# Sums and 1/std of four blocks kept in PSUM in the node stage, and half as many short memsets behind the early gathers

## The chip, the cores and the metric

The kernel runs on one core of a Trainium2 chip. A core has TensorE (PE, matrix products and transposes, results in the eight banks of PSUM), VectorE (DVE), ScalarE (ACT), GpSimd (POOL) and SyncE (SP), which run side by side and wait for one another on semaphores, and 16 DMA engines that all queues share. SP issues the plain transfers. GpSimd issues the indirect ones (a gather or a scatter of 128 rows by a list of row numbers). GpSimd and DMA reach SBUF, but not PSUM.

The metric is the time of one launch on the device in microseconds (us).

## The reference

The input is x (100000 nodes of 64 floats), 25000 edges with a source, a destination (sorted) and 64 features, and the weights. Everything is float32.

```
h = relu(layernorm(x))                               # (x - mean) / sqrt(var + 1e-5)
msg_f = mlp_f([h[src], h[dst], edge])                # 192 -> 128 -> 128, relu between
msg_r = mlp_r([h[dst], h[src], edge])
agg   = segment_sum(msg_f, dst) + segment_sum(msg_r, src)
out   = x + h + mlp_n([agg, h])                      # 192 -> 128 -> 64, relu between
```

## The kernel before

The second layer of both edge MLPs is multiplied into the first node weight, so a message is what an edge adds to the hidden layer of a node. A DRAM table holds one row of 128 floats per node: the node's share of its hidden layer, to which the edges' shares are then added.

**Node stage** (0 to about 286 us). 98 blocks ("windows" in the code) of 1024 nodes, 128 partitions by G = 8 nodes by 64 floats. For each, SP loads x into a ring of four buffers `nx` (256 KB), VectorE sums (`sum_begin`, L1056), subtracts the mean (`centre_begin`, L1063), sums the squares that ScalarE makes (`variance_begin`, L1069), inverts ScalarE's square root (`invert_begin`, L1073) and makes h (`normal_begin`, L1080). TensorE transposes h (L764) and multiplies it (L775), ScalarE copies the result out (L683), and SP stores it to the table (512 KB). VectorE's order in one step n is: sum of block n+3, variance of n+2, centring of n+3, inverse of n+2, h of n+2. The sums and 1/std of all blocks stay in SBUF, in `all_sums` and `all_rstd` (128 x 98 x 8), because the edge stage makes h of every block again on ScalarE (`h_window`, L639) from x, -mean/std and 1/std. The steps 4 to 91 are a hardware loop of 22 turns with four steps each.

Beside this GpSimd makes the **early gathers**: for the 98 batches of the edge stage, the x rows of all even batches and of the first three odd ones, 52 x 4 = 208 gathers of 128 rows (L514), into `got_even` and `got_odd`. Behind each of them stands a memset of 128 x 256 floats of `idle`, which is a part of `to_send[0]` (L567). In SBUF the gathers need only the list `gather_first`, so they start at 7.9 us and are issued one after the other, whatever the other engines do. The memset waits for the memset before it, and the two write nothing that anyone reads.

**Edge stage** (to about 1340 us). 98 batches of 256 edges. Per batch: layer norm of the gathered rows on VectorE and ScalarE, transposes (`turn`), first layer (`layer1`), second layer (`layer2`), `messages` on VectorE, `join` on TensorE (L846: adds the messages of a batch that go to the same node), a copy of the result to `to_send` on ScalarE (`copy_sums`, L625), and four scatters on GpSimd that add 128 rows each to the table (L532), with half of the gathers of a later odd batch behind them (L514 again). On TensorE a step is join of batch n-2, turn of n, layer2 of n-1, layer1 of n. On ScalarE a step is root n, relu n-1, half of h_window n, square n+1, copy_sums n-2, copy_turned n, the other half. So what stands behind `copy_sums` of batch 0 on ScalarE is `copy_turned` of batch 2, without which TensorE can't go on with layer1 of batch 2 and all behind it. And `copy_sums` of batch 0 waits for `join` of batch 0 and for all 208 memsets (`act.wait_ge(s_paused, KB * (PAIRS + LOOK))`, L624), since they write into its output. GpSimd's scatters stand behind all early gathers in its own queue.

**Output stage** (to the end). 98 blocks: table in, relu, second node layer, plus x + h, out.

VectorE's setup work in the node stage uses banks 6 and 7: the turned edge numbers (bank 6, L916), w2 turned (bank 7, L744 and L928) and the products of the weights (bank 6, L752 and L932). Banks 0 and 1 hold the transposes, 2 to 5 the products. Apart from the turned w2, bank 7 is not used before the first odd `join` of the edge stage.

## Time and profile before

| | us |
|---|---|
| median of 3 runs (1623.82 to 1632.91) | 1625.49 |
| time of the profiled execution | 1627.22 |
| its span, first to last instruction | 1625.5 |
| early gathers and their memsets, in the span | 7.9 to 339.3 |
| node stage, until its last product is copied out | about 0 to 283 |
| edge stage, from the first scatter to the last | 340.9 to 1354 |
| output stage | to 1625.5 |

Busy shares of the span: PE 81%, DVE 60%, ACT 58%, POOL 69%. They are means over three stages with different limits, so the rows below are read by stage. A row of a timeline gives the start and the length of an instruction in us, its engine, line, operation and operands, how many were merged (x), and in brackets how long its engine had been idle before and what ended that. "issue" is idle time for which the profile shows no releaser.

### The profile page before, as it was taken

To read this page: it belongs to the slowest core of one execution; us is meant where nothing else is said; L and a number is where in the kernel's file an instruction comes from. 1 tells how busy PE (TensorE), PEld (TensorE's weight loads), DVE (VectorE), ACT (ScalarE), POOL (GpSimd) and SP (SyncE) were. 2 spreads that over 40 slices of the span, in tenths; PEclk is the share of its full clock that TensorE was granted. 3 is DMA by queue.
4 is the path that set the end of the run, shared out by engine and by line. 5 is a ranking of instruction groups with operands and counts; after the bars stand their busy time and mean duration, and the time that the engine had idled before them with its cause. 6 is when DMAs were issued, how large, how long until landed. Compare 5 with 4: busy or idle time off the path is not lost.

```text
span 1625.5 us, 29085 instructions
## 1 busy us (share of the span) xinstructions
PE 1318.5 (81%) x7070; PEld 997.1 (61%) x7070; DVE 972.4 (60%) x2902; ACT 944.0 (58%) x2256; POOL 1120.1 (69%) x1003
## 2 busy tenths in 40 slices
PE   6988998457787788887877887878888865899998
PEld 4777776345565666665656665656666654666665
DVE  7999998336666666666665666666666641222222
ACT  5888888244555455555545555455555533677776
POOL 7899878888888888888888888888888862000000
PEclk9999999567878777778787778787777777999999
DMA  7999998335555555555545555555555546999998
GB/s 222 310 312 315 315 312 280 101 59 108 103 109 108 107 104 103 102 103 103 102 93 99 101 103 102 98 100 102 103 103 102 102 76 205 333 369 348 346 349 292
DMA packets 238374, 280.71 MB, mean 173 GB/s; under 512 B 53170, under 2 KB 155200, under 8 KB 238348
## 3 DMA queue, kind: packets, MB, share of 16 engines
q1 hardware_dynamic: 168408, 241.57, 44.7%
q0 software_dynamic: 68992, 38.59, 20.3%
q10 hardware_dynamic: 948, 0.30, 0.1%
q14 instruction: 21, 0.17, 0.0%
q8 instruction: 5, 0.08, 0.0%
HBM read 162.62 MB, written 117.72 MB: 172 GB/s over the span
## 4 chain that ended last, share of the span: by engine, by line
POOL 28%; issue 19%; DMA 15%; PE 9%; DVE 5%; ACT 1%; POOLq 0%; SPq 0%; DVEq 0%; another core or an unknown queue 0%; ACTq 0%
POOL table L532 24%; DMA out_x<-ncentred 12%; POOL got_odd L514 5%; DMA table<-to_send,scatter_at 3%; PE bank L846 3%; DVE ncentred L1137 2%; PE bank L820 2%; PE bank L818 2%; PE bank L833 1%; DVE same L979 1%; PE bank L871 1%; DMA same<-table 1%; PE bank L804 1%; PE bank L882 0%; DVE sums L961 0%
## 5 line engine op out<-in xcount | busy, mean ns | idle before, releaser
L532 POOL DMA_INDIRECT table<-to_send,scatter_at x392 | 640.9, 1635 | 134.1 <-issue 118.3
L846 PEld LDWEIGHTS bank<-message,same 128*128 128x128 f32 x1960 | 300.1, 243 | 47.1 <-issue 43.6
L846 PE MATMUL bank<-message,same 128*128 128x128 f32 x1960 | 322.4, 335 | 3.3 <-DVE message L1010 3.3
L639 ACT ACTIVATE nh<-nx,all_sums,all_rstd 128x64 f32<-128x64 f32 x784 | 280.2, 434 | 0.0
L514 POOL DMA_INDIRECT got_even<-in_x,gather_first x196 | 211.8, 1081 | 40.9 <-issue 36.1
L775 PE MATMUL bank<-wn_h,nturned 128*128 128x256 f32 x784 | 196.6, 394 | 26.9 <-ACT nhidden L683 18.4
L514 POOL DMA_INDIRECT got_odd<-in_x,gather_at x180 | 179.9, 999 | 54.8 <-issue 54.2
L818 PE MATMUL bank<-turned,w_ends 128*128 128x256 f32 x392 | 175.5, 540 | 37.8 <-ACT turned_edge L609 37.1
L804 PE MATMUL bank<-ident,h_ends 128*128 128x128 f32 x196 | 51.4, 355 | 184.4 <-DVE h_ends L1019 181.4
L1004 DVE TENSOR_TENSOR scatter_at<-moved,ids 128x4 int32<-128x4 f32 x98 | 16.0, 163 | 296.6 <-DMA table<-to_send,scatter_at 296.6
L775 PEld LDWEIGHTS bank<-wn_h,nturned 128*128 128x128 f32 x784 | 143.1, 192 | 63.3 <-issue 33.0
L820 PE MATMUL bank<-turned_edge,w_edge 64*128 64x256 f32 x392 | 179.4, 547 | 0.0
L991 DVE CUSTOM_DVE_ANT_0 junk<-same,earlier 128x128 bf16<-128x128 f32 (+3 forms) x392 | 168.9, 487 | 0.0
L713 ACT ACTIVATE nhidden<-bank,bn_col 128x512 f32<-128x512 f32 x196 | 124.0, 684 | 70.2 <-PE bank L871 70.2
L616 ACT ACTIVATE hidden<-bank,b 128x256 f32<-128x256 f32 x196 | 82.1, 470 | 124.3 <-PE bank L820 122.4
L979 DVE TENSOR_SCALAR same<-others,ids 128x128 f32<-128x128 int32 (+3 forms) x392 | 143.7, 429 | 11.7 <-issue 7.6
L804 PEld LDWEIGHTS bank<-ident,h_ends 128*128 128x128 f32 x196 | 28.9, 181 | 195.3 <-issue 195.3
L871 PE MATMUL bank<-ident,same 128*128 128x128 f32 x784 | 108.4, 282 | 38.1 <-DMA same<-table 36.5
L833 PE MATMUL bank<-w2n,hidden 128*128 128x128 f32 x784 | 139.0, 336 | 0.0
L625 ACT COPY to_send<-bank 128x512 f32<-128x512 f32 x98 | 56.6, 577 | 139.4 <-PE bank L846 55.7
L871 PEld LDWEIGHTS bank<-ident,same 128*128 128x128 f32 x784 | 85.4, 143 | 77.5 <-issue 53.7
L820 PEld LDWEIGHTS bank<-turned_edge,w_edge 64*128 64x128 f32 x392 | 75.1, 239 | 94.0 <-issue 94.0
(78 smaller groups left out, 1971.0 us busy)
## 6 DMA issues: line engine op xcount, KB each, us to landing
nx<-in_x SPq DMA_DIRECT2D x194, 256.0 KB
table<-nhidden SPq DMA_DIRECT2D x97, 512.0 KB
same<-table SPq DMA_DIRECT2D x97, 512.0 KB, 5.3
others<-numbers SPq DMA_DIRECT2D x196, 128.0 KB
out_x<-ncentred SPq DMA_DIRECT2D x97, 256.0 KB, 4.4
nx<-out_x SPq DMA_DIRECT2D x55, 256.0 KB, 4.6
out_x<-nh SPq DMA_DIRECT2D x31, 256.0 KB
table<-to_send,scatter_at POOLq DMA_INDIRECT x392
```

The source lines that it names most:

```text
L514: pool.indirect_dma_start(to[:, k * D:(k + 1) * D], None, x, bass.IndirectOffsetOnAxis(ap=numbers[:, k:k + 1], axis=0)).then_inc(landed, 16)
L532: pool.indirect_dma_start(table, bass.IndirectOffsetOnAxis(ap=scatter_at[s][:, k:k + 1], axis=0), to_send[s][:, k, :], None, compute_op=AL ...
L639: last = act.activation(nh[s][:, g, :], nx[place][:, g, :], ACT.Relu, bias=all_sums[:, at, g:g + 1].rearrange("p a g -> p (a g)"), scale=a ...
L713: act.activation(nhidden[s][:, odd * 512:odd * 512 + 512], bank[2 + 2 * s + odd][:, :], ACT.Relu, bias=bn1_col[:, 0:1]).then_inc(n_hidden[ ...
L775: last = pe.matmul(bank[2 + 2 * s + half][:, c:c + 2 * M], nturned[s][:, q * P:(q + 1) * P], wn1_h[:, :, :].rearrange("p a m -> p (a m)"), ...
L818: pe.matmul(bank[2 + s][:, c:c + JT * P], w1_ends[:, end, :], turned[s][:, 0:JT * P], start=True, stop=False)
L820: last = pe.matmul(bank[2 + s][:, c:c + JT * P], w1_edge[:, end, :], turned_edge[s][:, :], start=False, stop=True)
L833: last = pe.matmul(bank[4 + s][:, k * M:(k + 1) * M], hidden[s][:, end, j * P:(j + 1) * P], w2n[:, end, :], start=True, stop=True)
L846: last = pe.matmul(bank[6 + s][:, k * M:(k + 1) * M], same[s][:, o, k * P:(k + 1) * P], message[s][:, o, :], start=(o == k), stop=(o == KB ...
L871: last = pe.transpose(bank[2 + 2 * s + odd][:, q * P:(q + 1) * P], ntab[place][:, g * M:(g + 1) * M], ident[:, :])
L979: last = dve.tensor_scalar(same[s][:, o, 0:w], row[:, 0:w], ids[s][:, o:o + 1], None, ALU.is_equal)
L991: last = dve.tensor_tensor_reduce(junk[s][:, k, 0:w], same[s][:, k, 0:w], earlier[:, KB * P - w:], 1.0, 0.0, ALU.mult, ALU.add, before[s][ ...
```

## The change

VectorE writes the sums and 1/std of a block into one of four places in bank 7 (`some_sums`, `some_rstd`, 8 floats per partition each) instead of `all_sums` and `all_rstd`, and `centre_begin` and `normal_begin` read them there. Once in four blocks a copy (`keep`) moves 4 x 8 sums to `all_sums`, and another one 4 x 8 values of 1/std to `all_rstd`; two new semaphores count them, and the first of the next four blocks waits for them. The setup's turned w2 moves from bank 7 to bank 6, where its transposes wait for the copies of what lay there before. Of the memsets behind the early gathers every second one (k = 0 and 2) goes, and `copy_sums` waits for 104 instead of 208. The start of the edge stage waits for the 25 + 25 copies.

```diff
+        some_sums = bank[7][:, 0:NRING * G].rearrange("p (w g) -> p w g", g=G)
+        some_rstd = bank[7][:, NRING * G:2 * NRING * G].rearrange("p (w g) -> p w g", g=G)
...
+                    if k % 2 == 0:
+                        continue
                     if pauses:
                         pool.wait_ge(s_paused, pauses)
                     pool.memset(idle, 0.0).then_inc(s_paused, 1)
...
-                    act.wait_ge(s_paused, KB * (PAIRS + LOOK))
+                    act.wait_ge(s_paused, KB // 2 * (PAIRS + LOOK))
...
                 pe.wait_ge(s_params, 16 * N_PARAMS)
+                pe.wait_ge(s_setup_ev, 2)
                 for end in (SRC, DST):
-                    last = pe.transpose(bank[7][:, end * M:(end + 1) * M], w2[:, end, :], ident[:, :])
+                    last = pe.transpose(bank[6][:, end * M:(end + 1) * M], w2[:, end, :], ident[:, :])
...
             def sum_begin(i, s, turn, place):
                 dve.wait_ge(b_x[place], 16 * (turn + 1))
-                dve.tensor_reduce(of_window(all_sums, i, s), nx[place][:, :, :], AX.X, ALU.add).then_inc(b_sums[s], 1)
+                if place == 0 and not first(turn):
+                    dve.wait_ge(b_sums_kept, turn)
+                dve.tensor_reduce(some_sums[:, place, :], nx[place][:, :, :], AX.X, ALU.add).then_inc(b_sums[s], 1)
...
-                of_all = of_window(all_sums, i, s)
-                dve.scalar_tensor_tensor(out=ncentred[s][:, :, :], in0=of_all.to_broadcast([P, G, D]),
+                dve.scalar_tensor_tensor(out=ncentred[s][:, :, :], in0=some_sums[:, place, :].to_broadcast([P, G, D]),
                                          scalar=-1.0 / D, in1=nx[place][:, :, :], op0=ALU.mult, op1=ALU.add
                                          ).then_inc(b_centred[s], 1)
...
-            def invert_begin(i, s):
+            def invert_begin(i, s, turn, place):
                 dve.wait_ge(b_std[s], i + 1)
-                dve.reciprocal(of_window(all_rstd, i, s), nstd[s][:, :]).then_inc(b_rstd[s], 1)
+                if place == 0 and not first(turn):
+                    dve.wait_ge(b_rstd_kept, turn)
+                dve.reciprocal(some_rstd[:, place, :], nstd[s][:, :]).then_inc(b_rstd[s], 1)
...
                 dve.scalar_tensor_tensor(out=nh[place][:, :, :], in0=ncentred[s][:, :, :], scalar=0.0,
-                                         in1=of_all.to_broadcast([P, G, D]), op0=ALU.max, op1=ALU.mult
+                                         in1=some_rstd[:, place, :].to_broadcast([P, G, D]), op0=ALU.max, op1=ALU.mult
                                          ).then_inc(b_h[s], 1)
+
+            def keep(to, of, kept, w, k):
+
+                if 0 <= w.least(k) < NW:
+                    n = min(NRING, NW - w.least(k))
+                    dve.tensor_copy(to[:, bass.ds(w.number(k), n), :], of[:, 0:n, :]).then_inc(kept, 1)
...
                 w.do(centre_begin, 3, ring=NRING)
-                w.do(invert_begin, 2)
+                if w.n % NRING == 0:
+                    keep(all_sums, some_sums, b_sums_kept, w, 0)
+                w.do(invert_begin, 2, ring=NRING)
                 w.do(normal_begin, 2, ring=NRING)
+                if w.n % NRING == 1:
+                    keep(all_rstd, some_rstd, b_rstd_kept, w, -1)
...
+            dve.wait_ge(b_sums_kept, -(-NW // NRING))
+            dve.wait_ge(b_rstd_kept, -(-NW // NRING))
             for s in range(2):
-                dve.wait_ge(b_rstd[s], NW // 2)
                 dve.wait_ge(b_turn[s], NW // 2)
```

## Rows read from the trace of the kernel before

**Rows 1.** Busy time of each engine by stretch; columns in the first line.

```profile
core 0: us, PE busy (x) PEld busy (x) DVE busy (x) ACT busy (x) POOL busy (x), PEclk, DMA share, GB/s
20.00:270.00 250.00, 223.98 (x1113) 180.13 (x1112) 241.48 (x465) 215.14 (x460) 220.46 (x309) 0.99 0.91 310
...
303.00:339.00 36.00, 0.47 (x5) 0.27 (x3) 4.23 (x11) 0.00 (x0) 31.94 (x50) 0.54 0.18 46
341.00:1340.00 999.00, 807.53 (x3856) 614.22 (x3855) 623.51 (x2236) 509.03 (x1435) 814.39 (x570) 0.77 0.53 101
```

**Rows 2.** Waits, 285 to 345 us: engine, line, waited for, total, times, longest.

```profile
ACT to_send L625 <- POOL to_send L567: 40.8, 1, 40.8
```

**Rows 3.** Timeline where the edge stage begins: start, length, engine, line, instruction.

```profile
297.34 4.63 PE L846 MATMUL bank<-message,same 128*128 128x128 f32 x20
...
339.00 0.33 POOL L567 MEMSET to_send<- 128x256 f32 x1
...
339.42 0.58 ACT L625 COPY to_send<-bank 128x512 f32<-128x512 f32 x1 [40.83 <-POOL to_send L567]
...
340.86 1.64 POOL L532 DMA_INDIRECT table<-to_send,scatter_at  x1 [1.53 <-issue]
```

**Rows 4.** Timeline of one step of the node stage, VectorE and then GpSimd.

```profile
124.43 0.68 DVE L1063 SCALAR_TENSOR_TENSOR ncentred<-all_sums,nx 128x512 f32<-128x512 f32 x1
125.03 0.19 DVE L1073 RECIPROCAL all_rstd<-nstd 128x8 f32 x1
125.26 0.69 DVE L1080 SCALAR_TENSOR_TENSOR nh<-ncentred,all_rstd 128x512 f32<-128x512 f32 x1
125.96 0.69 DVE L1056 TENSOR_REDUCE all_sums<-nx 128x512 f32 x1
...
124.64 1.30 POOL L514 DMA_INDIRECT got_even<-in_x,gather_first  x1 [0.16 <-issue]
...
126.43 0.96 POOL L514 DMA_INDIRECT got_even<-in_x,gather_first  x1 [0.16 <-issue]
```

**Rows 5.** Groups, 0 to 290 us, by form: busy, mean ns, idle before.

```profile
L514 POOL DMA_INDIRECT got_even<-in_x,gather_first x163 | 179.7, 1102 | 35.6 <-issue 30.7 <-DVE gather_first L919 4.9
```

**Rows 6.** Groups, 300 to 340 us, when VectorE and TensorE stand still.

```profile
L514 POOL DMA_INDIRECT got_even<-in_x,gather_first x27 | 25.9, 958 | 4.4 <-issue 4.4
```

**Rows 7.** Timeline of the edge stage: two scatters and VectorE's instruction beside each.

```profile
875.77 0.69 DVE L1010 TENSOR_TENSOR message<-bank,b2n 128x512 f32<-128x512 f32 x1
...
875.80 1.57 POOL L532 DMA_INDIRECT table<-to_send,scatter_at  x1 [0.31 <-issue]
...
845.59 0.68 DVE L1048 TENSOR_TENSOR nsquares<-nx,nh 128x512 f32<-128x512 f32 x1
...
845.62 2.07 POOL L532 DMA_INDIRECT table<-to_send,scatter_at  x1 [0.30 <-issue]
```

**Rows 8.** Timeline of GpSimd: a gather right behind a gather, in the edge stage.

```profile
349.99 0.98 POOL L514 DMA_INDIRECT got_odd<-in_x,gather_first  x1 [0.30 <-issue]
```

**Rows 9.** Timeline of GpSimd: the first early gather, and the one long gap.

```profile
7.86 1.57 POOL L514 DMA_INDIRECT got_even<-in_x,gather_first  x1 [4.89 <-DVE gather_first L919]
...
238.27 0.97 POOL L514 DMA_INDIRECT got_even<-in_x,gather_first  x1 [4.72 <-issue]
```

**Rows 10.** Timeline of VectorE, edge stage: PSUM input, two SBUF inputs, a small one.

```profile
303.50 0.69 DVE L1010 TENSOR_TENSOR message<-bank,b2n 128x512 f32<-128x512 f32 x1 [3.48 <-PE bank L833]
304.11 0.68 DVE L1048 TENSOR_TENSOR nh<-nx,nh 128x512 f32<-128x512 f32 x1
...
305.04 0.15 DVE L1004 TENSOR_TENSOR scatter_at<-moved,ids 128x4 int32<-128x4 f32 x1
305.11 0.41 DVE L961 TENSOR_REDUCE sums<-got_even 128x4 f32<-128x256 f32 x1
```

**Rows 11.** DMA queues, 20 to 270 us: packets, MB, share of 16 engines.

```profile
q0 software_dynamic: 4927, 5.05, 7.7%
```

**Rows 12.** Waits, 20 to 270 us, of ScalarE for stores: total, times, longest.

```profile
ACT nhidden L683 <- DMA table<-nhidden: 3.8, 2, 2.9
```

More of the change, by code:

```diff
@@ L268, in gnn_layer @@
         b_rows = sems("b_rows_ready")
+        b_sums_kept = sem("b_sums_kept")
+        b_rstd_kept = sem("b_rstd_kept")
         b_stored = sems("b_rows_stored")
@@ L927, in copy_turned_weights @@
                 dve.wait_ge(s_setup_pe, 2)
-                dve.tensor_copy(w2t[:, :, :].rearrange("p a m -> p (a m)"), bank[7][:, 0:2 * M]).then_inc(s_setup_ev, 1)
+                dve.tensor_copy(w2t[:, :, :].rearrange("p a m -> p (a m)"), bank[6][:, 0:2 * M]).then_inc(s_setup_ev, 1)
             def copy_weight_products():
@@ L1048, in add_h @@
                 dve.tensor_tensor(to, nx[place][:, :, :], nh[s][:, :, :], ALU.add).then_inc(e_xh[s], 1)
-            def of_window(a, i, s):
-                return a[:, bass.ds(2 * i + s, 1), :].rearrange("p a g -> p (a g)")
             def sum_begin(i, s, turn, place):
                 dve.wait_ge(b_x[place], 16 * (turn + 1))
-                dve.tensor_reduce(of_window(all_sums, i, s), nx[place][:, :, :], AX.X, ALU.add).then_inc(b_sums[s], 1)
+                if place == 0 and not first(turn):
+                    dve.wait_ge(b_sums_kept, turn)
+                dve.tensor_reduce(some_sums[:, place, :], nx[place][:, :, :], AX.X, ALU.add).then_inc(b_sums[s], 1)
             def centre_begin(i, s, turn, place):
@@ L1069, in variance_begin @@
                 dve.tensor_reduce(nvar[s][:, :], nsquares[s][:, :, :], AX.X, ALU.add).then_inc(b_var[s], 1)
-            def invert_begin(i, s):
+            def invert_begin(i, s, turn, place):
                 dve.wait_ge(b_std[s], i + 1)
-                dve.reciprocal(of_window(all_rstd, i, s), nstd[s][:, :]).then_inc(b_rstd[s], 1)
+                if place == 0 and not first(turn):
+                    dve.wait_ge(b_rstd_kept, turn)
+                dve.reciprocal(some_rstd[:, place, :], nstd[s][:, :]).then_inc(b_rstd[s], 1)
             def normal_begin(i, s, turn, place):
                 dve.wait_ge(b_rstd[s], i + 1)
-                of_all = of_window(all_rstd, i, s)
                 if not first(turn):
@@ L1104, in _ @@
                         edge_columns()
-                    Step(NW, 0).do(invert_begin, k)
+                    Step(NW, 0).do(invert_begin, k, ring=NRING)
                     Step(NW, 0).do(normal_begin, k, ring=NRING)
```

## The prediction

> **What bounds the kernel now.** I read the busy time by stretch first, because the shares of the whole span mix three stages. In the node stage VectorE is busy 241.48 of 250 us [rows 1], so VectorE sets the pace there. In the edge stage GpSimd is busy 814.39 of 999 us [rows 1], and between its indirect DMAs lie 0.30 us each in which nothing else is waited for [rows 7, 8]. With those, one batch takes GpSimd four scatters and two gathers, about 10.3 us, and 98 batches take about 1010 us, so this stage is GpSimd's queue from end to end. Between the two lies the stretch that the change is about: from 303 to 339 us TensorE is busy 0.47 us, ScalarE 0.00 and GpSimd 31.94 of 36 [rows 1]. I then ask who waits for whom there. ScalarE's copy to to_send (L625) waits 40.8 us for GpSimd's memset (L567) [rows 2]. The timeline shows the same in order: the first join ends at 297.34 + 4.63 = 301.97, the last memset at 339.33, the copy starts at 339.42 and the first scatter at 340.86 [rows 3]. All engines had the edge stage under way and stopped for the early gathers. If those end sooner, the copy and everything behind it move forward, until the copy meets its other condition, the end of the first join. This is at most 339.4 - 302.0 = 37.4 us.
>
> So two dates count: **P**, when GpSimd is through with the early gathers, and **J**, when the first join is done (302.0 now). The copy starts at the later of the two.
>
> **GpSimd, the memsets.** A step is now a gather of 0.96, the memset of 0.33 directly behind it, and 0.16 of issue ahead of the next gather [rows 3, 4]. Without the memset, a gather follows a gather 0.30 us after its end and takes 0.98 [rows 8]. So a memset that goes doesn't save its 0.33: it saves 0.33 + 0.16 - 0.30 - 0.02 = 0.17 us. 104 of them are 17 us. (The mean length of all 104 together would say 34; the row in which two gathers follow one another is the one that counts.) Both ends: 0, if the gap grew until it eats the memset, and 34, if the gather followed without the gap. Even 0 would leave P at 315, by the next paragraph.
>
> **GpSimd, the gathers themselves.** Beside a standing VectorE a gather takes 958 ns, 27 of 27 [rows 6]. Up to 290 us the mean is 1102 ns over 163 [rows 5]: 163 x 0.144 = 23.5 us more than at rest, and with the 12 into got_odd at about the same some 25. The timeline says which ones pay. The gather at 124.64 starts inside the centring (124.43 to 125.11) and takes 1.30; the one at 126.43 starts inside a reduction (125.96 to 126.65) and takes 0.96 [rows 4]. I went through all 157 gathers from 20 to 275 us: the 94 that start outside L1063 and L1080 take 0.96, every one, and of the 63 that start inside one of these two nearly all take 1.2 to 1.5: what is left of VectorE's instruction at their start, and 0.83 (for the one at 124.64, 0.47 + 0.83). L1063 and L1080 are the instructions with two inputs in SBUF. The edge stage shows the case that the change makes: a scatter that starts 0.03 us into L1048, with two SBUF inputs, takes 2.07; one that starts 0.03 us into L1010, of the same size but with one input in PSUM, takes 1.57, as at rest [rows 7]. After the change L1063 and L1080 have one input in PSUM, and the reductions never held a gather up. So I take the whole 25 us for gone, less about 1 us for gathers that fall beside the first batches of the edge stage. Bounds: 0 (nothing is freed) to 25.
>
> The Trainium skill, "SBUF — State Buffer", section "Who interferes with whom", has a rule on this: VectorE with two SBUF inputs contends with a GpSimd instruction that reads SBUF, and with at most one such input, outside its two-port modes, it doesn't. By that rule rival B below is excluded altogether, whichever of the two inputs is in SBUF. The trace agrees for the one form of which it has such pairs, L1010 against L1048 [rows 7].
>
> **P** is then 339.3 - 17 - 24 = 298 us. From below it can be checked by building it up: start 7.9 [rows 9], 104 pairs of 0.96 + 0.30 + 0.98 + 0.33 + 0.16 = 2.73, that is 284, the one gap of 4.7 [rows 9]: 297. P is thus ahead of J even now.
>
> **VectorE, which sets J.** J moves by what the node stage grows. VectorE has 24.5 turns of four blocks. Per turn:
> - Eight two-input instructions read PSUM. L1010 with a PSUM input is 0.69 long and the next starts 0.61 later; two inputs in SBUF give 0.68 [rows 10] and 0.60 (L1063, 124.43 to 125.03) [rows 4]. Eight times 0.01 is 0.08 us.
> - Two copies of 32 elements. A four-element instruction is followed after 0.07 us by the next (305.04 to 305.11), a 512-element one after 0.60 [rows 4], so an element is 1.04 ns and 32 of them 0.10 us. As nobody waits for the copies but sums three instructions on, the step counts and not the length. Two are 0.20 us. Far bound: their full length of about 0.18, 0.36 for two.
> - Eight small outputs (sums and 1/std) go to PSUM. No row of VectorE shows an output in PSUM. A gain has no ground, since the same number of elements is written. The far bound is another fixed part of an instruction, 0.07 each [rows 10], 0.54 in all, mostly through L1080, which waits for L1073 and starts 0.23 behind it [rows 4]. I take 0.01 each, the price of the PSUM input, which is the nearest row: 0.08.
>
> Together 0.36 us per turn, 9 us in the stage, 7 to 24 between the bounds. VectorE gets about 1 us back: in some windows L1080 is 0.72 long instead of 0.69, where a gather had started first. So J goes from 302 to 310 (308 to 325). ScalarE (215.14 of 250) and TensorE (223.98) [rows 1] have room and are not the bound. What is queued behind the new waits on VectorE is its whole next step, but both wait for a copy that was issued two or more instructions earlier. The move of w2 to bank 6 and its wait lie at 25 us, once, beside other work, and cost nothing that is left at 300 us; uncovered it would be under 1 us.
>
> The Trainium skill, "VectorE: DVE Perf Modes", section "The TRN2 errata", speaks against the change: it gives 58 cycles for an SBUF source and 120 for a PSUM source, 62 cycles or 65 ns more per instruction. The row shows 10 ns for a full-width PSUM input [rows 10]. By the page's figure on all 18 accesses a turn would grow by some 1.4 us; what the same mechanism would do here is rival C.
>
> **DMA.** The gathers' queue takes 7.7% of the 16 engines over 250 us for 155 gathers [rows 11], 0.12 us each. Some 25 more gathers fall into the node stage, 3 us of DMA time, which moves the share of 0.91 [rows 1] to 0.92. I cost it at nothing; the cover is the lead of the four buffers, and ScalarE's waits for stores are 3.8 us in the stage [rows 12].
>
> **Sum.** The copy starts at the later of 298 and 310, so at 310 instead of 339.4: 29.4 us sooner. What follows is the same sequence, at about the granted clock of 0.54 that TensorE has there now [rows 1], and then GpSimd's queue, which shifts as a whole. The profiled execution took 1627.2 us, so 1597.8; the median of the runs lies 1.7 lower, which gives 1596.1. I say 1597. With J from 302 (all of VectorE's added work hidden) to 325 the same sum gives 1590 to 1613.
>
> **Rivals.**
> - **A, the forecast**: GpSimd is freed and J decides. 1590 to 1613, 1597 likeliest.
> - **B, the gathers are not freed**: the remaining SBUF input could occupy the shared way all the same, above all in L1063, where it is the second input. Against it stands the undisturbed scatter beside L1010, whose SBUF input is also the second; for it, that this is a scatter, and few such cases exist. Then P = 339.3 - 17 = 322, later than J, and the time is 1627.2 - 17 = 1610.
> - **C, PSUM is dear**: each of the 18 accesses to PSUM, the copies' among them, costs a further fixed part of 0.07: with the copies' own 0.20 this is 1.5 us per turn, 36 us in the stage, J = 337. Time 1627.2 - 2.4 = 1625. For it: the write is not shown. Against: rows 10.
> - **D, slower**: the gathers come every 1.36 us instead of every 1.59, in front of the blocks' loads and stores, in DMA engines that are busy for 0.91 of the time. ScalarE once waited 2.9 us for a store [rows 12]. If such a stall came once per turn, it would cost 24.5 x 2.9 = 71 us and the time would be 1669. It decides from 13 such stalls on (29.4 + 8.1 us). Against it: 3 us of added DMA work, and only two waits of this kind in 250 us now [rows 12].
> - **E, no gain**: P and J move as said, but the edge stage gives it back, because a wait on the scatters or the transfers and not GpSimd's queue sets its end, or the memset's absence is paid in the gathers themselves. Against it: the first batch goes at the stage's usual pace at once, its second gather starting 9.1 us behind its first scatter [rows 3, 8]. Time 1627.
>
> **How the numbers follow.** A 0.74, B 0.12, C 0.07, D 0.04, E 0.03. A measurement of this kernel tells about 0.5%, 8 us, from no change. Faster by more than that: A and B, 0.86. Within: C and E, 0.10. Slower: D, 0.04. The range goes over A and B, 1589 to 1613; C, D and E, 0.14, stay outside.
>
> **What the profile would show.** Gathers of 0.96 and 0.98 throughout the node stage, in pairs 0.30 apart, and the last memset near 298; if their mean stays at 1.10, B is right. The steps of VectorE in the node stage: L1073 to L1080 still near 0.23, L1080 to the next near 0.61, the copies 0.10; a turn longer by 0.36 us. The wait of L625 for GpSimd gone, with TensorE's join as its releaser near 310, and the first scatter near 311.5. The edge stage, first scatter to last, as long as before. A share of DMA waits on L683 or L1056 in the node stage beyond 10 us would make D right.

## The result: 12% slower in two groups of runs, 2% faster in a third

The changed kernel took 1828.24 us (median of 4 runs, 1821.79 to 1831.88) beside 1629.2 for the kernel before: ratio 1.1228, 95% interval 1.1201 to 1.1254. The forecast was 1597 and wrong, in sign too. The same file, run twice more beside the experiments, took 1826.66 (ratio 1.1189, 1.1137 to 1.1241) and **1593.79** (one run, before 1630.60 beside it). So there are two courses of one kernel, and the runs come in groups: what ran in one group, on one chip and close together, took the same course all along. In one course the node stage nearly stands still while the early gathers run, and I call it the standing course. In the other it runs as before. First the standing course.

The busy time by stretch of the changed kernel, columns as in [rows 1]:

```profile
20.00:270.00 250.00, 64.01 (x196) 48.05 (x194) 43.91 (x90) 34.71 (x76) 200.10 (x271) 0.59 0.25 75
303.00:512.00 209.00, 187.74 (x924) 150.60 (x924) 203.26 (x424) 180.95 (x385) 0.00 (x0) 0.99 0.82 286
536.00:1546.00 1010.00, 809.10 (x3856) 614.00 (x3855) 628.50 (x2251) 509.24 (x1436) 821.39 (x575) 0.77 0.54 101
```

The first row answers to the first of [rows 1]: VectorE was busy 241.48 of 250 us and is now busy 43.91. Only GpSimd works on, with the gathers at the distance that was forecast (1.35 us). From 303 us, when its queue is empty, VectorE is at 203.26 of 209 again. The edge stage is as long as before. So the node stage stood while the early gathers ran, and some 5 us longer. Of the 98 blocks 19 were made by 280 us (98 before). The rest took 216 us after the gathers, 2.7 each, the normal pace.

The end of the wait, timeline as in [rows 3]:

```profile
532.11 2.50 PE L853 MATMUL bank<-message,same 128*128 128x128 f32 x20
534.64 0.58 ACT L631 COPY to_send<-bank 128x512 f32<-128x512 f32 x1 [1.28 <-PE bank L853]
536.09 1.64 POOL L536 DMA_INDIRECT table<-to_send,scatter_at  x1 [239.28 <-ACT to_send L631]
```

The copy now follows the join, as forecast, but at 534.6 us and not 310. GpSimd waited 239 us for it. The copy is 195.2 later than in [rows 3], and 1625.5 + 195.2 = 1820.7, where the new span is 1820.1. So this delay is the whole loss.

What the node stage waited for, 20 to 300 us: engine, line, waited for, total, times, longest.

```profile
ACT nturned L682 <- remote: 214.7, 13, 35.6
DVE bank L1080 <- issue: 202.3, 12, 35.1
PE bank L782 <- ACT nhidden L689: 143.3, 11, 33.4
DVE w2t L935 <- remote: 4.1, 1, 4.1
```

ScalarE's copy of TensorE's transposes is the first in the ring: VectorE waits for the root that stands behind this copy on ScalarE, TensorE for ScalarE's results. "remote" says that no instruction ended then to which the profile could ascribe the release. One step shows it:

```profile
47.49 0.98 PE L771 MATMUL bank<-ident,nh 128*128 128x128 f32 x4
...
80.17 0.59 ACT L682 COPY nturned<-bank 128x512 f32<-128x512 f32 x1 [35.60 <-remote]
80.65 1.08 ACT L689 COPY nhidden<-bank 128x512 f32<-128x512 f32 x2
81.60 0.32 ACT L676 ACTIVATE nstd<-nvar,eps 128x8 f32<-128x8 f32 x1
...
81.96 0.21 DVE L1080 RECIPROCAL bank<-nstd 128x8 f32<-128x8 f32 x1 [35.07 <-issue]
...
85.42 0.80 PE L771 MATMUL bank<-ident,nh 128*128 128x128 f32 x4
...
110.19 0.58 ACT L682 COPY nturned<-bank 128x512 f32<-128x512 f32 x1 [27.75 <-remote]
```

Transposes of two blocks alternate between two semaphores. Those at 47.49 are the ones that the copy at 110.19 reads. An instruction that others wait for adds one to a semaphore when it ends, and this is its increment. These transposes ended at 48.5, and the record of the semaphore that they increment is at 110.17: **61.7 us late**. The records of the semaphores are in the trace beside the instructions, and I took for each one in the node stage the time since the end of the instruction that increments it (20 to 300 us):

```
                             TensorE's increments        GpSimd's        ScalarE's,   semaphore records
                             seen  over 0.1  longest     longest         VectorE's    in the whole trace
changed kernel, 1828 us        30     30      61.7 us      4.4 us        0.01 us      20,983
kernel before, profile shown  140     27       0.45        0.01          0.01         20,368
changed kernel, 1594 us       198      0       0.02        0.01          0.01         32,274
```

What TensorE computes is done in time, and the news of it is late. The last late records of the node stage come at 301.03 to 301.24 us: four within 0.2 us, for work that was done between 3 and 33 us before, so they arrive as if they had been held up together. From then on none is late there. Not every increment has a record: of TensorE's in this stretch 30 of 36 in the first row, 140 of 199 in the second and 198 of 198 in the third. The second row is the surprise: in the profile from which I forecast, 27 of 140 were already up to 0.45 us late, which the third kernel of the table doesn't show at all. And the number of semaphore records in a trace has two values, of which more below.

### The profile page after: what moved, and what is told of

It reads as the page before. It is cut to its first block, busy times and chain, and to the rows that moved or that the text cites. A ratio compares the mean times of both kernels' runs of the same rounds, so it can differ in the third digit from the quotient of the medians.

```text
span 1820.1 us, 28926 instructions
## 1 busy us (share of the span) xinstructions
PE 1342.8 (74%) x7070; PEld 1012.0 (56%) x7070; DVE 976.1 (54%) x2952; ACT 943.5 (52%) x2256; POOL 1057.5 (58%) x899
## 4 chain that ended last, share of the span: by engine, by line
issue 32%; POOL 25%; DVE 13%; DMA 13%; PE 10%; another core or an unknown queue 5%; ACT 2%; DVEq 1%; POOLq 0%; SPq 0%; ACTq 0%
POOL table L536 21%; DMA out_x<-ncentred 10%; POOL got_odd L518 4%; DVE ncentred L1068 2%; PE bank L853 2%; DVE nvar L1074 2%; DMA table<-to_send,scatter_at 2%; PE bank L827 2%; DVE ncentred L1154 2%; PE bank L825 2%; PE bank L840 1%; DVE bank L1062 1%; DVE same L986 1%; DVE nh L1086 1%
## 5 line engine op out<-in xcount | busy, mean ns | idle before, releaser
L782 PE MATMUL bank<-wn_h,nturned 128*128 128x256 f32 x784 | 219.7, 429 | 233.5 <-ACT nhidden L689 166.3
L782 PEld LDWEIGHTS bank<-wn_h,nturned 128*128 128x128 f32 x784 | 157.4, 211 | 276.3 <-issue 173.4
L518 POOL DMA_INDIRECT got_even<-in_x,gather_first x196 | 187.3, 955 | 53.5 <-issue 48.4
L682 ACT COPY nturned<-bank 128x512 f32<-128x512 f32 x98 | 56.0, 572 | 248.6 <-remote 221.0
L1080 DVE RECIPROCAL bank<-nstd 128x8 f32<-128x8 f32 x98 | 19.8, 202 | 233.4 <-issue 202.3
```

The lines of the kernel that those rows point to most:

```text
L518: pool.indirect_dma_start(to[:, k * D:(k + 1) * D], None, x, bass.IndirectOffsetOnAxis(ap=numbers[:, k:k + 1], axis=0)).then_inc(landed, 16)
L782: last = pe.matmul(bank[2 + 2 * s + half][:, c:c + 2 * M], nturned[s][:, q * P:(q + 1) * P], wn1_h[:, :, :].rearrange("p a m -> p (a m)"), ...
```

## The experiments

The kernels ran in six groups, each group on one chip, with the kernel before timed beside (its medians 1628.5 to 1633.1 in all groups, whichever course the others took). The table puts them together with the first result. "Distance" is the median time from one early gather to the next, taken over pairs (with two numbers where a kernel changes its pattern). In e2 it leaves out most of the hold-ups by VectorE: with them its mean is 1.43. The mean of e4 is 1.43 as well, in part because its memsets waited for late increments of the memsets before them (19 times, 21.3 us). The kernel before has 1.45 from an undisturbed gather to the next [rows 4], and 1.59 in the mean. "Records" are the semaphore records in the trace. The chip of the first result is not on record.

```
group  chip  kernel                      distance   first join   time us   records
0       ?    changed                      1.35        534.6      1828.2     20,983
1      10    e1 PSUM alone                1.45        302.5      1600.9     32,401
             e2 half the memsets alone    1.36        301.8      1595.6     32,264
             e3 long memsets              1.46        302.6      1603.1     32,320
2       9    e4 short memsets             1.28        533.5      1822.4     20,657
             e5 no memsets, SBUF          1.26        555.5      1846.7     20,803
             e6 320 columns               1.38        525.7      1818.6     20,560
             e7 only the sums in PSUM     1.35        545.3      1838.1     20,793
3       4    e8 384 columns               1.405       528.3      1816.5     20,695
             e9 a quarter of each row     1.35        553.5      1842.4     20,787
             e10 64 rows                  1.31        551.3      1839.6     20,769
4       1    e11 dense later              1.45, 1.35  302.5      1597.1     32,313
             e12 dense first              1.35, 1.45  303.2      1601.3     32,340
             e13 224 columns behind each  1.42        301.2      1603.3     32,398
             e14 none at first            1.26, 1.36  300.6      1594.1     32,231
5       9    e15 changed, again           1.35        302.9      1593.8     32,274
             e16 e11 again                as e11      307.2      1597.1     32,373
6       4    e17 changed, timed           1.35        537.2      1826.7     20,927
             e18 e2 again                 as e2       521.1      1803.9     20,806
```

### The two halves, and other lengths of the memset

**e1_psum_alone** undoes the memsets' part: one behind each early gather, as before.

```diff
-                    if k % 2 == 0:
-                        continue
...
-                    act.wait_ge(s_paused, KB // 2 * (PAIRS + LOOK))
+                    act.wait_ge(s_paused, KB * (PAIRS + LOOK))
```

> The PSUM half of the change alone: sums and 1/std in bank 7, with the memset behind each of the 208 early gathers as before. In the changed kernel TensorE's semaphore increments reached ScalarE 10 to 60 us late as long as the early gathers ran, and the node stage stood. Theory M (the memsets are the gaps that let the increments through, and with half of them there are too few): this kernel is sound, the gathers take 0.96 each, the last memset ends near 8 + 208 x 1.45 + 5 = 314, and the time is 1600 to 1610. Theory V (the gathers held up by VectorE are the gaps, and without the hold-ups there are none): this kernel is as slow as the changed one, 1780 to 1830. If both count, something between, 1650 to 1750.

Measured: 1600.94, ratio 0.984 (0.981 to 0.9869), the node stage undisturbed.

**e2_half_memsets_alone** is the kernel before with the memsets' part: the same lines the other way round.

> The memset half of the change alone: a memset behind every second early gather, with the sums and 1/std in SBUF as before. Theory M (too few memsets): slow, 1750 to 1830, node stage standing while the gathers run. Theory V (VectorE's hold-ups are the gaps): sound, gathers still held up by VectorE, the last memset near 322, time 1610.

Measured: 1595.55, ratio 0.9793 (0.9762 to 0.9824). So each half alone was a gain beside the kernel before, of 1.6 and 2.1%, and I took the loss for something that only both together make.

**e3_long_memsets** keeps 104 memsets and makes them 512 columns long.

```diff
-        idle = to_send[0][:, 0:2, :].rearrange("p k m -> p (k m)")
+        idle = to_send[0][:, 0:4, :].rearrange("p k m -> p (k m)")
```

> The changed kernel with each of its 104 memsets over 512 instead of 256 columns (0.6 instead of 0.33 us): the same share of time in memsets as before, in half as many pauses. If the length of a pause decides whether TensorE's increments get through, the node stage runs and the time is 1600 to 1650. If it is their number or the pause behind each gather, it stays at 1780 to 1830.

Measured: 1603.07, ratio 0.9846 (0.9808 to 0.9884). Together the three said that a mean distance somewhere between 1.35 and 1.43 us upsets the node stage.

### Period, pauses, VectorE's operands

**e4_short_memsets** is e1 with memsets of 64 columns.

```diff
+        idle = to_send[0][:, 0, 0:64]
```

> The changed kernel's PSUM half, with a memset behind each early gather, but over 64 instead of 256 columns (some 0.17 us by the 0.33 and 0.55 us of 256 and 512 columns). A gather then comes every 0.96 + 0.17 + 0.16 = 1.29 us, which is denser than in the changed kernel (2.70 per pair, 1.35 each) but never two without a pause between. Rate theory (TensorE's increments starve once the gathers come oftener than about every 1.36 us on average): slow, 1780 to 1830. Pause theory (a pause behind each gather lets them through, however dense): sound, early gathers end near 280, the first join near 302.5 decides, 1586 to 1592. Phase theory (the period of 2.70 us meets the node stage's own of about 2.7): sound as well, since the period is another.

Measured: 1822.36, ratio 1.1185 (1.1157 to 1.1214), 32 of the 34 TensorE increments seen over 0.1 us late, up to 38 us. A pause behind each gather isn't enough.

**e5_no_memsets_sbuf** is the kernel before without the memsets and without the wait for them. **e6_memsets_320** is the changed kernel with 320 instead of 256 columns. **e7_only_sums_in_psum** takes 1/std back into SBUF:

```diff
-        some_rstd = bank[7][:, NRING * G:2 * NRING * G].rearrange("p (w g) -> p w g", g=G)
+        some_rstd = sb("some_rstd", [P, NRING, G])
```

> The kernel before with no memset at all behind the early gathers, sums and 1/std in SBUF. A gather comes every 1.25 us plus VectorE's hold-ups. Rate theory and pause theory: slow, 1780 and more. If VectorE's hold-ups alone are enough to let TensorE's increments through: sound, early gathers end near 285, time 1585 to 1592. Phase theory: sound.

> The changed kernel with its 104 memsets over 320 instead of 256 columns: 0.055 us longer, the pair of gathers every 2.76 instead of 2.70 us, 1.38 each. Between the changed kernel (256 columns, standing) and the one with 512 (sound). Rate or pause theory with a threshold: either sound at 1600, or standing at 1780 to 1830, or, if the starving is gradual, in between at 1650 to 1750. Phase theory: sound, 1600.

> The changed kernel with only the sums in PSUM and 1/std in a small SBUF buffer, so that one of VectorE's two instructions per block (the one that makes h) still holds a gather up, and the memset is behind every second gather. If any hold-up that comes now and then breaks the starving: sound, early gathers end near 305, time 1595. If half of them are not enough: 1700 to 1830.

Measured: 1846.71, 1818.55 and 1838.07. e5 has nothing of the PSUM part and stands all the more. It differs from the kernel before by the memsets alone, and that one took 1628.5 us in the same group. The waits of e5, 20 to 300 us, for its copy of the transposes:

```profile
ACT nturned L670 <- remote: 251.0, 8, 53.9
```

So the PSUM part isn't needed for the standing, and leaving out the memsets is enough. But e5 shows too that the lateness doesn't end with the gathers. Its last gather, and the next instruction on any engine:

```profile
276.08 0.95 POOL L514 DMA_INDIRECT got_even<-in_x,gather_first  x1 [0.30 <-issue]
289.98 0.59 ACT L670 COPY nturned<-bank 128x512 f32<-128x512 f32 x1 [29.93 <-remote]
```

The last early gather landed at 278.2, and from 280 to 289 no engine worked and the DMA engines moved nothing. Still the copy waited until 289.98 for an increment that was 59.6 us late, and the one at 301.2 was 38 us late. In the other standing kernels the last late record of the node stage comes 2.4 to 6.3 us behind the end of the last gather, here 24.4. So the lateness isn't made only at the moment in which a gather is issued or under way: something that has piled up goes on.

**e8_memsets_384** (384 columns, 1.405 us) was to place the limit, which I expected near 1.385.

> The changed kernel with its 104 memsets over 384 instead of 256 columns, 0.11 us longer: a pair of gathers every 2.81 us, 1.405 each. So far kernels with a gather every 1.26, 1.28, 1.35 and 1.38 us stood, those with one every 1.39 (memsets halved, sums in SBUF), 1.45 and 1.46 ran. Rate theory (the mean distance of the gathers decides, the bound is near 1.385): sound, early gathers end near 305, the first join near 302.5, time 1590 to 1594, faster than every kernel so far. If VectorE's hold-ups and not the mean distance made the kernel with 1.39 run: standing, 1810.

Measured: 1816.48, ratio 1.1151 (1.1122 to 1.1179), standing above that limit.

### What a gather moves

**e9_quarter_rows** and **e10_64_rows** change what the early gathers fetch; GpSimd first clears their targets, which takes until 17.6 us.

```diff
+            quarters = x.rearrange("n (a d) -> (n a) d", d=16)
...
+                pool.indirect_dma_start(to[:, k * D:k * D + 16], None, quarters,
...
+                pool.indirect_dma_start(to[0:64, k * D:(k + 1) * D], None, x,
+                                        bass.IndirectOffsetOnAxis(ap=numbers[0:64, k:k + 1], axis=0)
```

> The changed kernel with early gathers that fetch 16 instead of 64 floats per row (the rest of their output is set to zero once on GpSimd before the first gather, some 10 us, so the edge stage computes with wrong rows). The number of gathers and rows and their pace stay, the bytes fall to a quarter. If the bytes or the DMA engines' time are what blocks TensorE's increments: sound, 1600. If it is the issue of the gathers, or of their rows: standing, 1820.

> The changed kernel with early gathers of 64 instead of 128 rows (the other half of their output is set to zero once on GpSimd before the first gather, some 10 us, so half the edges compute with wrong rows). If GpSimd needs less time for a gather of 64 rows, the gathers come even denser, while the rows per us fall. If rows (descriptors) per us decide, with the bound near 128 rows per 1.385 us: sound, 1590 to 1600. If the number of gathers per us decides: standing, 1800 or more.

Measured: 1842.41 and 1839.55. Both stand: neither a quarter of the bytes nor half of the rows is few enough to prevent it. Together with the DMA share of 0.25 while the node stage stands, rival D's reason (gathers in front of the blocks' transfers in full DMA engines) is out.

### The theory of the distance falls

After ten kernels my theory was: a mean distance of 1.405 us or less makes TensorE's increments late, 1.433 and more doesn't. Four kernels were to say where the limit lies and whether the start or the steady state decides.

**e13_224_behind_each** is e1 with 224 columns. In **e11_dense_later** the changed kernel's pattern begins after 60 gathers, in **e12_dense_first** it ends there; **e14_none_at_first** is e2 without any memset behind the first 40.

```diff
+        idle = to_send[0][:, 0:2, :].rearrange("p k m -> p (k m)")[:, 0:224]
...
+                    if gathers > 60 and k % 2 == 0:
+                        continue
...
+                    if gathers <= 60 and k % 2 == 0:
+                        continue
...
+                    if gathers <= 40 or k % 2 == 0:
+                        continue
```

> The sums and 1/std in PSUM, and a memset of 224 instead of 256 columns behind each early gather. By the 256 and 64 columns behind each (1.446 and 1.28 us per gather) this gives 1.42 us per gather, between the slowest distance that has stood (1.405, 384 columns behind every second) and the fastest that ran (1.446, not counting the 1.433 of the kernel with VectorE's operands in SBUF). Theory M (the mean distance of the early gathers decides, and the limit lies between 1.405 and 1.433): either result is possible and places the limit; if it runs, the gathers end at 7.9 + 208 x 1.42 = 304 us, the first join at 302 to 303, the first scatter at about 306, and the time is 1591 to 1595. If it stands: 1815 to 1825. A node stage that runs at half speed, or a time between 1610 and 1800, would speak against M, by which it is all or nothing.

> The changed kernel, but the first 60 of the early gathers have a memset behind each (1.446 us per gather, until about 95 us), and the other 148 behind every second only (1.35). Theory S (the start decides: the node stage must come through its first blocks, the steady distance afterwards doesn't matter): no standing, gathers through at 95 + 200 = 295 us, first join at about 303 to 310, time 1590 to 1600. Theory M (the steady distance decides): sound until about 95 us, with 30 blocks done or so, and TensorE's increments late from then until the gathers end at about 295; the first join near 295 + the 68 blocks that are left x 2.6 = 475 us, time about 1765.

> The changed kernel, but only the first 60 of the early gathers have a memset behind every second (1.35 us per gather, until about 89 us), and the other 148 behind each (1.446). Theory M: TensorE's increments late until about 90 us and sound afterwards at once; gathers through at 89 + 214 = 303 us, the first join some 60 to 70 us later than 302, at 360 to 375, time 1650 to 1670. Theory H (once it stands it stays so until the gathers end, a state that keeps itself up): the node stage stands until 303 us, time 1820 to 1845.

> The kernel before with a memset behind every second early gather only (operands in SBUF, which runs), but none at all behind the first 40 gathers, which then come 1.25 us apart until about 58 us, and not yet held up by much of VectorE. The question is why that kernel runs, although its undisturbed steps are 1.355 apart. Theory F (VectorE's hold-ups and its own pace keep each other up: as long as VectorE runs it slows the gathers to 1.43, and once it stands nothing does, so the same kernel has two courses): once standing, it goes on standing at 1.355 until the gathers end at about 58 + 168 x 1.355 = 286 us, time 1820 to 1850. Theory M alone, with TensorE's increments punctual again as soon as a memset stands behind every second gather: recovery at about 60 us, a loss of 40 to 50 us, time 1640 to 1650. If the first 40 don't make it stand at all: 1590 to 1600, and the start alone is no trigger.

Measured: 1603.25 (ratio 0.9817, 0.9793 to 0.9841), 1597.12, 1601.33 and 1594.12. None stood, not even e14 with 40 gathers like these (GpSimd's timeline), the densest there can be:

```profile
29.76 0.95 POOL L514 DMA_INDIRECT got_even<-in_x,gather_first  x1 [0.30 <-issue]
31.02 0.95 POOL L514 DMA_INDIRECT got_even<-in_x,gather_first  x1 [0.30 <-issue]
32.28 0.95 POOL L514 DMA_INDIRECT got_even<-in_x,gather_first  x1 [0.30 <-issue]
```

By the distance e11 should have taken about 1765 us. And e12 is the changed kernel until 89 us: the same instructions in the same order at the same times, to 0.13 us, on all engines until 24 us. Then in the changed kernel ScalarE's copy waits 5.1 us for the transposes, and in e12 it doesn't wait at all. First the changed kernel, then e12, ScalarE's timeline:

```profile
28.21 0.59 ACT L682 COPY nturned<-bank 128x512 f32<-128x512 f32 x1 [5.11 <-remote]
```

```profile
25.63 0.57 ACT L683 COPY nturned<-bank 128x512 f32<-128x512 f32 x1
```

Nothing that the two programs had done by then explains that. But I now saw that in each group all kernels had taken the same course, so that the group and the distance could not be told apart.

### The same kernel, twice more

**e15_after_again** and **e17_after_timed** are the changed kernel without any edit, **e16_dense_later_again** is e11 and **e18_half_memsets_again** is e2.

> The changed kernel, unchanged, once more. The last four kernels (1.35 to 1.45 us per gather in all orders) all ran, and e12_dense_first is the same as the changed kernel for its first 60 gathers, instruction by instruction at the same times up to 24 us, where the changed kernel's first increment was late and its own was not. The kernels were run in groups, each group on another chip: e1 to e3 on one, e4 to e7 on a second, e8 to e10 on a third, e11 to e14 on a fourth, and all of a group ran or all stood. Theory K (the chip decides: on some, dense gathers make TensorE's increments late, on others not): this run takes 1590 to 1600 us on a chip of the one kind, and 1820 to 1832 on one of the other. Theory M (the pattern of the gathers decides, whatever the chip): 1820 to 1832 here, always.

> e11_dense_later once more (60 gathers with a memset behind each, 1.446 us per gather, then 148 with one behind every second, 1.35), on the same chip as e15_after_again. Theory K, if that one takes about 1597: this one too. If that one stands, this one tells whether 1.446 us is far enough on such a chip: increments punctual until about 95 us and late afterwards, time 1750 to 1780 (the limit lies between 1.35 and 1.446); or late from the start, 1820 to 1835 (it lies above 1.446, and the two halves of the change were a gain only on the chip that they were tried on).

> The changed kernel, unchanged, a third time. It took 1828 us in one group of runs and 1594 in another, and that one was on the very chip on which e4 to e7 had stood. So what differs lies in the group of runs (all kernels of one group share it, and the kernel before, timed beside them, takes 1629 to 1633 in all), and not in the kernel and not in the chip alone. Either this group is sound: 1592 to 1600, ratio 0.977 to 0.984, the first join at 302 to 308. Or it stands: 1820 to 1832. A value between, or one that changes from round to round, would speak against a property of the whole group.

> e2_half_memsets_alone again (VectorE's operands in SBUF, a memset behind every second early gather), beside e17_after_timed. If that one is sound: 1593 to 1600 for both, within 0.5% of one another, since GpSimd is through at about 306 here and at 294 there, but the first join ends at 302 in both. If that one stands, this one tells whether the half alone is safe there: 1593 to 1600 if the mean distance of 1.43 us is enough, 1820 to 1850 if it isn't, in which case only the kernel before with its 1.59 us is known to be safe.

Measured: e15 1593.79 and e16 1597.07, both undisturbed; e17 1826.66 (1.1189) and e18 1803.92, both standing. The four runs of e18 went from 1780.32 to 1811.58, and its ratio is that of the two shorter ones, 1.0953 (1.0892 to 1.1014). The busy time of e15, e17 and e18 in the same stretch:

```profile
20.00:270.00 250.00, 220.01 (x1097) 177.20 (x1097) 240.60 (x503) 213.69 (x455) 203.57 (x273) 0.99 0.92 311
```

```profile
20.00:270.00 250.00, 58.76 (x184) 44.65 (x182) 41.25 (x85) 32.48 (x71) 200.80 (x271) 0.59 0.26 73
```

```profile
20.00:270.00 250.00, 78.20 (x269) 59.92 (x267) 59.62 (x112) 48.81 (x106) 202.47 (x266) 0.64 0.32 95
```

GpSimd does the same in all three (203.57, 200.80, 202.47 us); VectorE is at 240.60, 41.25 and 59.62. Three things follow.

- **The group decides, and not the chip alone**: chip 9 had e4 to e7, which stood, and then e15, which didn't. Chip 4 had e8 to e10 and e17 and e18, all standing. Which of a chip's cores a group ran on isn't on record, so that may be what differs.
- **The halves of the change aren't safe either**: e2, a gain of 2.1% in group 1, is a loss of 9.5% in group 6. There it differs from the kernel before, 1631.5 us beside it, by half of the memsets alone. So in such a group the memsets behind the gathers keep the node stage going. e1 was tried in no group of that kind.
- **The groups differ in their traces**: every trace of a standing group has 20,560 to 20,983 semaphore records, every one of the others 32,231 to 32,401, at the same number of instructions (28,926 in the changed kernel each time). Most of those that are missing are records of DMA landings: 16,539 to 16,926 against 27,113 to 27,193. The trace of the kernel before that stands ahead of the prediction has 20,368, so it is of the standing kind, in which that kernel doesn't stand. In this kind TensorE's increments are late in the edge stage too (600 to 1000 us: 15 of 114 in e17, up to 1.9 us, and 5 of 104 in the kernel before, up to 1.65; none of 153 in e15).

What is shown is the path of the loss (gathers closer together, TensorE's increments late, ScalarE's copy waiting). What stays open is what holds the increments up, what makes a group of the one or of the other kind, and whether the missing records and the late increments have one cause. One rival in particular is untested: that the recording itself holds the increments up in such a group. Every timed run was recorded with a span and a granted clock, so whether an increment is late where nothing is recorded isn't known. Nor was it tried whether e1, e3 or e13 run in a group of the standing kind, or e5 in one of the other, or where the limit lies: in the standing kind every kernel with a median distance of 1.405 us or less stood, and the kernel before, with 1.45 and its hold-ups, has only the 0.45 us of the table. The mean is no sharper: e4 stood with the 1.43 at which e2 ran in group 1.

## Why the prediction was wrong, point by point

**"Two dates count"** held in both courses: the copy starts at the later of P and J, here with the end of the join (the 1.28 us in its row are the time that ScalarE had been idle). I gave P's movement 17 + 24 us and J's 8, and the sum was right in form. What failed is J, because the node stage depends on GpSimd's queue through more than VectorE and DMA: P came at 296.8 and J at 534.6, forecast 298 and 310.

**P, the memsets** (17 us) **and the gathers** (24 us): right. GpSimd in e15, between 120 and 124 us:

```profile
120.27 0.95 POOL L518 DMA_INDIRECT got_even<-in_x,gather_first  x1 [0.30 <-issue]
121.21 0.33 POOL L573 MEMSET to_send<- 128x256 f32 x1
121.70 0.96 POOL L518 DMA_INDIRECT got_even<-in_x,gather_first  x1 [0.16 <-issue]
```

A pair takes 2.70 us (2.73 forecast), and the group of [rows 5] reads, with VectorE at full speed beside it:

```profile
L518 POOL DMA_INDIRECT got_even<-in_x,gather_first x193 | 185.6, 962 | 53.7 <-issue 48.9 <-DVE gather_first L926 4.8
```

1102 ns have become 962. P, the end of the last memset, was 294.4 in e15 and 296.8 in the standing course, forecast 298. Most of the 4 us between 294.4 and 298 are the pairs' 0.03 us, 104 times. Rival B is out. The Trainium skill, "SBUF — State Buffer", section "Who interferes with whom", says that a VectorE instruction with at most one SBUF input, outside the 2-port modes, does not contend with GpSimd. By that rule all hold-ups go, and in e15 they went: of the gathers between 20 and 275 us none took over 1 us.

**J, VectorE's own work** (8 us): mechanism right, size too large. e15's VectorE, in order, to be read against [rows 4]:

```profile
121.52 0.20 DVE L1080 RECIPROCAL bank<-nstd 128x8 f32<-128x8 f32 x1
121.75 0.69 DVE L1086 SCALAR_TENSOR_TENSOR nh<-ncentred,bank 128x512 f32<-128x512 f32 x1
122.36 0.18 DVE L1094 COPY all_rstd<-bank 128x32 f32 x1
122.46 0.68 DVE L1062 TENSOR_REDUCE bank<-nx 128x8 f32<-128x512 f32 x1
123.05 0.68 DVE L1074 TENSOR_REDUCE nvar<-nsquares 128x8 f32<-128x512 f32 x1
123.64 0.68 DVE L1068 SCALAR_TENSOR_TENSOR ncentred<-bank,nx 128x512 f32<-128x512 f32 x1
```

The copies take 0.10 each, as worked out. The 16 other accesses, for which I took 0.16 per turn, cost nothing that can be seen: over the stage the median step behind the sum is 0.596 in both kernels, behind the centring 0.598 (0.599 before), behind h 0.605 (0.610), behind the reciprocal 0.236 (0.230). A turn grew by 0.15 us in the mean (10.87 to 11.02), forecast 0.36, and the last block by 3.4 us. The first join ended at 302.9 in e15, where I had 310 (302.0 in [rows 3]), so the term for the growth of J, 8 us, measured 0.9. That is why e15 is faster than forecast. Rival C is out: the page "VectorE: DVE Perf Modes" of the Trainium skill, section "The TRN2 errata", gives 58 cycles for an SBUF source and 120 for a PSUM source, 62 more, and the rows above show no part of them.

**The sum**, from the copy to the end: 1286.1 us before, 1285.4 in the standing course, 1289.2 in e15. Rival E is out. In e15 the copy moved by 36.5 us and the end by 33.4, so the stages behind it gave back 3.1, which I had at nothing.

**DMA, "I cost it at nothing"**: right as far as DMA goes (0.91 became 0.92 in e15), and the wrong place to look. Rival D had the right sign and the right trigger, gathers at 1.36 instead of 1.59, with the wrong mechanism, and a price of 71 us where J came 233 us later. I gave it 0.04 because the only path that I saw between GpSimd's queue and the node stage was the DMA engines. **The step that failed is this**: I worked J out as 302 us plus VectorE's own added work less a microsecond, 310, and put what the denser gathers do to the node stage at nothing beyond DMA. Behind that stood the belief that an engine which waits for nobody can take no time from those that don't wait for it, unless they share DMA engines or a port. In its place the runs showed J at 534.6, with TensorE's increments up to 61.7 us late and ScalarE's copy of the transposes waiting 214.7 us for them. What holds them up stays open.

Could the profile of before have said so? In part. Its waits in the edge stage have this row, which I passed over (whole span):

```profile
ACT to_send L625 <- remote: 9.9, 7, 1.5
```

Seven times TensorE's join was done and ScalarE's copy, behind it, learned it 1.6 to 1.9 us later, by the records of the join's semaphore (1.5 is the longest idle time before the copy). In e1 and e15 no wait on "remote" exists. In the standing course the same row reads:

```profile
ACT to_send L631 <- remote: 14.7, 11, 1.5
```

It names no size and no limit, so a loss of 12% could not be worked out from it. But it says that in this trace TensorE's increments weren't punctual, while GpSimd issued indirect DMAs, and the change makes those denser. That deserved a rival with a wide range, and the range 1589 to 1613 had no room for it. In a group of the other kind the forecast of 1597 would have stood against 1593.8, partly because two errors offset each other: J was 7 us too late, and the 3 us that came back behind it were left out.

## What to carry to other kernels

Pauses between indirect DMAs on GpSimd that look like waste can be what keeps the other engines in time: take them away only with a run in which the semaphores are watched, and in more than one group of runs, since here one group showed a gain of 2% and the next a loss of 12% of the same file. A "remote" wait behind a finished TensorE instruction is the sign to look for, before and after. And when all experiments of one sitting agree, repeat the unchanged kernel in another: ten kernels gave me a sharp limit that didn't exist.

## What the runs showed of the hardware that I had not expected

- TensorE's increments can arrive up to 61.7 us (e5: 83.6) behind the work while GpSimd issues gathers 1.26 to 1.405 us apart, in some groups of runs; GpSimd's own by up to 4.4 (its memset at 121.41 waited 0.80 for the increment of the memset before); ScalarE's and VectorE's by no more than 0.01 wherever a record shows them. They become punctual again 2.4 to 6.3 us after the last gather, in e5 24.4 us after it, with 9 us between in which no engine and no DMA engine worked.
- On one chip (9) e4 to e7 stood in one group, and in another the changed kernel and e11 ran undisturbed. The number of semaphore records in the trace tells which kind of group it was, before one looks at any time.
- A gather on GpSimd costs nearly the same whatever it moves. With 128 rows of 64 floats it takes 0.95 to 0.96 us in the changed kernel. These are the groups of e9 (16 floats per row) and e10 (64 rows), 20 to 290 us:

```profile
L525 POOL DMA_INDIRECT got_even<-in_x,gather_first x181 | 172.7, 954 | 44.9 <-issue 44.9
```

```profile
L523 POOL DMA_INDIRECT got_even<-in_x,gather_first x181 | 165.9, 917 | 44.8 <-issue 44.8
```

- In the standing node stage TensorE's granted clock is 0.59 in the mean instead of 0.99 (first row of the result against [rows 1]), with the engine busy 64 of 250 us instead of 224.
